# Int16 weight transposes moved from TensorE to a DMA queue in a pre-norm decoder layer

## The reference, cut to what matters

```python
x = x + attn(layernorm(x))                    # 16 query heads, 4 key/value heads, head size 16, rope, causal
x = x + cross(layernorm(x), ctx, mask)        # softmax(x ctx^T / 16, masked) @ ctx
xq  = quant_dequant(layernorm(x))             # per row: round(v / s) * s, s = max|v| / 127
gu  = xq @ quant_dequant(w_gate_up).T         # w_gate_up 1408 x 256, scale per output row
h   = silu(gu[..., :704]) * gu[..., 704:]
out = x + quant_dequant(h) @ quant_dequant(w_down).T    # w_down 256 x 704, scale per output row
```

## Time and profile before

| | us |
|---|---|
| median of three runs | 101.81 |
| lowest and highest of them | 101.38, 102.7 |
| the profiled execution | 102.22 |
| its span, first to last instruction | 100.4 |
| mean granted TensorE clock | 0.988 |

### The profile page before, as it was taken

The page is one execution under the profiler, slowest core; times in us unless marked ns, Lnnn a source line. Parts: engine busy times, 40 slices in busy tenths (PEclk is TensorE's granted clock), DMA queues, the critical chain, the costliest instruction groups (busy, mean ns, idle before and its releaser), DMA issues.

```text
span 100.4 us, 2487 instructions
## 1 busy us (share of the span) xinstructions
PE 92.1 (92%) x834; PEld 71.3 (71%) x834; DVE 75.4 (75%) x217; ACT 65.1 (65%) x175; POOL 61.5 (61%) x130
## 2 busy tenths in 40 slices
PE   5999699989999999999999999998999999999560
PEld 4788479766867787867877797776887977775220
DVE  5135979828999998697696669797878696998731
ACT  1403210489978677777787879689777897988420
POOL 5476666179922755976188674882489992872220
PEclk9999999999999999999999999999999999999995
DMA  2999999930000000000000000000000010021121
GB/s 35 368 342 421 416 407 415 351 98 3 0 7 3 0 3 0 7 0 0 7 0 0 0 0 7 3 0 0 0 0 0 7 52 3 0 104 52 52 104 52
DMA packets 4521, 8.34 MB, mean 83 GB/s; under 512 B 349, under 2 KB 3358, under 8 KB 4382
## 3 DMA queue, kind: packets, MB, share of 16 engines
q1 hardware_dynamic: 4272, 7.96, 21.6%
q10 hardware_dynamic: 238, 0.23, 0.7%
HBM read 7.15 MB, written 1.05 MB: 82 GB/s over the span
## 4 chain that ended last, share of the span: by engine, by line
PE 72%; DVE 13%; POOL 6%; issue 3%; ACT 3%; DVEq 0%; ACTq 0%; POOLq 0%
PE ps_s L456 11%; PE ps_r L263 8%; PE ps_q L304 6%; PE ps_y L538 4%; PE ps_r L290 4%; PE ps_y L372 3%; POOL gate_up L1169 3%; PE ps_r L399 3%; PE ps_s L352 3%; PE ps_s L328 3%; PE ps_x L388 2%; PE ps_q L312 2%; PE ps_y L364 2%; PE ps_s L339 2%; PE ps_s L482 2%
## 5 line engine op out<-in xcount | busy, mean ns | idle before, releaser
L1169 POOL TENSOR_TENSOR gate_up<-gate,up_row 128x704 f32<-128x704 f32 x7 | 11.9, 1699 | 6.6 <-ACT gate L738 5.0
L263 PE MATMUL ps_r<-warm 128*128 128x256 bf16 x58 | 9.5, 330 | 1.0 <-DVE warm L786 1.0
L1144 POOL TENSOR_TENSOR rot_c<-rot,b_rope 128x128 f32<-128x128 f32 x8 | 3.6, 456 | 9.1 <-DVE rot L861 9.1
L263 PEld LDWEIGHTS ps_r<-warm 128*128 128x128 bf16 x58 | 6.7, 120 | 3.1 <-DVE warm L786 1.0
L456 PE MATMUL ps_s<-gate_hi,x_int_T 128*128 128x352 f32 x28 | 7.7, 355 | 0.0
L884 DVE RECIPROCAL y_rsum<-ps_y 128x128 f32<-128x128 f32 x8 | 7.6, 950 | 0.1
L1200 POOL TENSOR_TENSOR y_out<-ffn,x_aug 128x256 f32<-128x256 f32 x7 | 4.8, 690 | 4.4 <-DVE ffn L1040 4.4
L538 PE MATMUL ps_y<-w_T,h_T 128*128 128x256 bf16 (+1 forms) x42 | 6.5, 275 | 0.9 <-DVE ffn L1040 0.8
L456 PE MATMUL ps_s<-up_int,x_int_T 128*128 128x352 f32 x32 | 6.8, 335 | 0.1
L456 PE MATMUL ps_s<-gate_lo,x_int_T 128*128 128x352 f32 x28 | 6.8, 323 | 0.0
L749 ACT ACTIVATE h_int<-hid,h_inv 128x704 int16<-128x704 f32 x7 | 6.1, 877 | 0.3 <-DVE h_inv L1035 0.3
(11 more groups left out here) (197 smaller groups left out, 290.6 us busy)
## 6 DMA issues: line engine op xcount, KB each, us to landing
ctxT<-in_ctxT SPq DMA_DIRECT2D x1, 1024.0 KB, 8.7
w_raw<-in_w SPq DMA_DIRECT2D x2, 512.0 KB, 11.2
ctx_aug<-in_ctx SPq DMA_DIRECT2D x1, 1024.0 KB, 17.1
out_x<-y_out SPq DMA_DIRECT2D x8, 128.0 KB, 1.7
x_aug<-in_x SPq DMA_DIRECT2D x1, 768.0 KB, 7.0
xT<-in_xT SPq DMA_DIRECT2D x1, 768.0 KB, 9.9
w_raw<-in_w SPq DMA_DIRECT2D x1, 704.0 KB, 14.8
x_first<-in_x_first SPq DMA_DIRECT2D x1, 416.0 KB, 4.5
```

The source lines that it names most:

```text
L263: nc.tensor.matmul(ps_r[:, 0:2 * T], warm[:, 0:P], warm[:, :], start=True, stop=True)
L1169: nc.gpsimd.tensor_tensor(gate_up[j % 2][:, :, :], gate[j % 2][:, :, :], up_row[:, :].rearrange("p (i f) -> p i f", i=2), ALU.mult).then_i ...
```

## The change

- SP's DMA queue transposes W1 and W2 with `dma_start_transpose`, block by block, as int16 (w1_int) and as bf16 (w2_bf). `transpose_gate`, `transpose_up`, `transpose_w2` and the spreads leave TensorE.
- The scales of W1 and W2 are stored as a row in DRAM and loaded back to all partitions by a broadcasting load.
- The gate half: GpSimd's new `scale_gate` widens the transposed integers and multiplies them with the row; `upper_gate` and `lower_gate` then work on SBUF, in two halves. gate_T and the row lie in the memory of w1_raw, so the last `quantise_w1` must be over before they are written.
- GpSimd's new `widen_w2` turns w2_int into bf16, after one memset of w2_bf.
- The context means use 8 columns in place of 60 and come in two halves of four sequences. One `keep_warm(7)` goes, another uses the bank ps_x.
- All five lists have a new order.

```diff
-    GT = -(-FF // P)
-    CM = 61
+    GT = FF // P
+    CM = 9
...
             sp.dma_start(ctx_aug[:, :, 0:D], ctx_in).then_inc(s["ctx_loaded"], 16)
+            done(sp, "w1_scale_done", len(W1_PARTS) - 1)
+            sp.dma_start(w1_row_dram.rearrange("(o p) -> p o", p=P), w1_scale[:, :], allow_slow_non_contiguous=True).then_inc(s["w1_row_stored"], 16)
+            done(sp, "w1_int_ready", 2)
+            sp.dma_start_transpose(w1_T[:, 0:GT + 1, :, :].rearrange("p o c t -> p (o c) t"),
+                                   w1_int[:, 0:GT + 1, :].rearrange("p o d -> p (o d)")).then_inc(s["gate_T_loaded"], 16)
+            done(sp, "w1_int_ready", 4)
+            sp.dma_start_transpose(w1_T[:, GT + 1:WT, :, :].rearrange("p o c t -> p (o c) t"),
+                                   w1_int[:, GT + 1:WT, :].rearrange("p o d -> p (o d)")).then_inc(s["up_T_loaded"], 16)
+            sp.wait_ge(s["w1_row_stored"], 16)
+            sp.dma_start(w1_row[:, :], w1_row_dram.unsqueeze(0).to_broadcast([P, 2 * FF])).then_inc(s["w1_row_loaded"], 16)
+            done(sp, "w2_scale_done", 0)
+            sp.dma_start(w2_row_dram.rearrange("(c p) -> p c", p=P), w2_scale[:, :], allow_slow_non_contiguous=True).then_inc(s["w2_row_stored"], 16)
+            sp.wait_ge(s["w2_row_stored"], 16)
+            sp.dma_start(w2_row[:, :], w2_row_dram.unsqueeze(0).to_broadcast([P, D])).then_inc(s["w2_row_loaded"], 16)
+            for c in range(DC):
+                done(sp, "w2_bf_ready", c)
+                sp.dma_start_transpose(w2_T[:, :, c * P:(c + 1) * P], w2_bf[:, c, :]).then_inc(s[f"w2_T_{c}_loaded"], 16)
             for j in range(B):
...
+            def upper_gate(c):
+                done(act, "gate_T_ready", c)
+                nc.scalar.copy(gate_hi[:, c, :], gate_T[:, c, :]).then_inc(s["gate_hi_ready"], 1)
+            def evacuate_up(c):
+                act.wait_ge(s["gate_T_loaded"], 16)
+                act.wait_ge(s["up_T_loaded"], 16)
+                nc.scalar.copy(up_int[:, c, 0:FL], w1_T[:, GT, c, FL:P])
+                nc.scalar.copy(up_int[:, c, FL:FF].rearrange("p (o t) -> p o t", t=P), w1_T[:, GT + 1:WT, c, :]).then_inc(s["up_int_ready"], 1)
...
+            def lower_gate(c):
+                done(dve, "gate_T_ready", c)
+                done(dve, "gate_hi_ready", c)
+                nc.vector.tensor_tensor(gate_lo[:, c, :], gate_T[:, c, :], gate_hi[:, c, :].bitcast(F32), ALU.subtract).then_inc(s["gate_lo_ready"], 1)
...
+            def scale_gate(c):
+                done(pool, "w1_int_ready", 4)
+                pool.wait_ge(s["gate_T_loaded"], 16)
+                pool.wait_ge(s["w1_row_loaded"], 16)
+                nc.gpsimd.tensor_copy(gate_T[:, c, 0:GT * P].rearrange("p (o t) -> p o t", t=P), w1_T[:, 0:GT, c, :])
+                nc.gpsimd.tensor_copy(gate_T[:, c, GT * P:FF], w1_T[:, GT, c, 0:FL]).then_inc(s["gate_T_widened"], 1)
+                done(pool, "gate_T_widened", c)
+                nc.gpsimd.tensor_tensor(gate_T[:, c, :], gate_T[:, c, :], w1_row[:, 0:FF], ALU.mult).then_inc(s["gate_T_ready"], 1)
+            def widen_w2(c):
+                done(pool, "w2_int_ready", c)
...
+                nc.gpsimd.tensor_copy(w2_bf[:, c, 0:FF], w2_int[:, c, :]).then_inc(s["w2_bf_ready"], 1)
```

More of the change, by code:

```diff
@@ L287, in mean_ctx, with mean_ctx_half @@
                 pe.wait_ge(s["ctxT_loaded"], 16)
-                for j in range(B):
+                mean_ctx_half(0)
+            def mean_ctx_half(half):
+                means = ps_r[:, 0:B * CM].rearrange("p (b n) -> p b n", n=CM)
+                for j in range(half * B // 2, (half + 1) * B // 2):
                     for c in range(DC):
@@ L532, in down @@
                     done(pe, "x1_ready", B - 1)
-                    done(pe, "w2_ready", DC - 1)
+                    for c in range(DC):
+                        pe.wait_ge(s[f"w2_T_{c}_loaded"], 16)
                 bank_free(pe, "ffn_ready", j)
@@ L559, in _ @@
             pe.wait_ge(s["warm_ready"], 1)
[L560 to L563, removed]
-            transpose_gate(1, "gate_lo_ready", 0); transpose_q_max(1); mask_other_keys(1); transpose_qk(2)
@@ new lines, in _ @@
+            rotate_sum(4); residual_2(0); max_scores(3); amax_x(0); invert_sums(2); max_cross(1)
+            step_x(0); invert_x(0); normalise_y(2); bias_cross(1); rotate(5); residual_1(2); invert_cross_sum(1)
+            rotate_sum(5); max_scores(4); invert_sums(3); lower_gate(0); residual_2(1); normalise_y(3)
+            amax_x(1); max_cross(2); bias_cross(2); rotate(6); step_x(1); invert_x(1); residual_1(3)
+            invert_cross_sum(2); rotate_sum(6); max_scores(5); invert_sums(4); lower_gate(1); normalise_y(4)
@@ new lines, in _ @@
+            residual_2(2); max_cross(3); bias_cross(3); amax_x(2); step_x(2); invert_x(2); residual_1(4)
+            rotate(7); max_scores(6); invert_cross_sum(3); rotate_sum(7); invert_sums(5); residual_2(3)
+            normalise_y(5); max_cross(4); bias_cross(4); residual_1(5); max_scores(7); invert_cross_sum(4)
+            amax_x(3); invert_sums(6); normalise_y(6); step_x(3); invert_x(3); max_cross(5); bias_cross(5)
+            residual_1(6); residual_2(4); invert_cross_sum(5); amax_x(4); step_x(4); invert_x(4); invert_sums(7)
@@ new lines, in _ @@
+            finish_gate(0); residual_2(5); max_cross(6); bias_cross(6); normalise_y(7); amax_x(5)
+            invert_cross_sum(6); step_x(5); invert_x(5); residual_1(7); finish_gate(1); residual_2(6)
+            max_cross(7); bias_cross(7); hidden(0); amax_h(0); amax_x(6); scale_h(0); invert_h(0); hidden(1)
+            step_x(6); invert_x(6); amax_h(1); invert_cross_sum(7); scale_h(1); invert_h(1); hidden(2)
+            residual_2(7); amax_h(2); amax_x(7); scale_h(2); invert_h(2); step_x(7); invert_x(7); hidden(3)
@@ L1081, in _ @@
+            add_residual(7)
         @block.gpsimd
@@ L1097, in _ @@
             pool.wait_ge(s["v_zero"], 1)
+            nc.gpsimd.memset(w2_bf[:, :, :], 0.0).then_inc(s["w2_bf_zero"], 1)
             nc.gpsimd.memset(v_pad[:, :, :, DH:DH + 1], 1.0).then_inc(s["ones_ready"], 1)
@@ new lines, in _ @@
+            scale_rope(3); centre_x(3); centre_x(4); centre_x(5); scale_rope(4); scale_rope(5); centre_ctx(0)
+            centre_x(6); rstd_2(0); centre_ctx(1); rotate_c(3); scale_rope(6); centre_x(7); centre_ctx(2)
+            centre_ctx(3); rotate_c(4); scale_gate(0); rstd_2(1); centre_ctx(4); scale_rope(7); rotate_c(5)
+            scale_gate(1); rstd_2(2); rotate_c(6); whole_x2(0); centre_ctx(5); widen_w2(0); rstd_2(3)
+            centre_ctx(6); widen_w2(1); rotate_c(7); rstd_2(4); scale_x(0); whole_x2(1); scale_x(1); whole_x2(2)
```

258 lines of the change are left out of this document (82 added, 176 removed).

## The result

| us | before | after |
|---|---|---|
| median of four runs each, same chip | 102.25 | 108.09 |
| lowest and highest | 101.38, 103.34 | 107.79, 110.67 |
| ratio of the times, 95% interval | | 1.060 [1.050, 1.070] |

The change makes the kernel 6% slower. The forecast was 98.2 with a range of 94.8 to 105.5: wrong in sign and outside the range. The profile of after is of its longest run, 110.67, with a mean granted clock of 0.883; the others (spans 106.0 to 106.6) have 0.896 to 0.923, so its rows carry 2 to 3 us more than the median.

A forecast was written before the change was run, and what follows sets the result against it. TensorE, busy 92% of the span, was taken as the bound between 30 and 90 us. Profiled 102.2 - 0.3 (lead at rotate(5)) - 4.0 (TensorE) + 0.5 (GpSimd) = 98.4, adjusted to the runs' median 98.2; range 94.8 to 105.5.

The forecast's parts named there:

- Part 1: Start, until rotate(3): less TensorE work puts rotate(2) near 18.8; lead of 3.0 us at rotate(3) and rotate(4).
- so 0.3 us: In the start: context-mean products of 8 columns in place of 60, bounded between nothing and 1.6 us, taken to save 0.3.
- Part 2: GpSimd in the middle: 5.9 us more work, not the bound by its sum; by its order rotate(5) starts near S + 4.2.
- S: Start of scale_gate(0) on GpSimd: forecast 33.5, break-even 33.8, every microsecond above that lost one for one.
- Part 3: When S is, by scale store, transposes and row load in SP's queue: low end 31, high end 39.7, taken as 33.5.
- rival B: Transposes or 4-byte store late, S near 39.7, rotate(5) 5.9 us late: 104.6 us, deciding from S = 39.3; chance 0.25.
- rival A: Everything on time: S = 31, rotate(5) at 35.2, lead 2.8 us, time 95.9 us; chance 0.16.
- Part 4: From rotate(5) to the end: TensorE loses 4.0 us of pieces, 0.5 us given back for GpSimd's added blocks.
- All of them pieces of the chain: After rotate(5): TensorE's removed spreads, up transposes and w2 transposes lie on the chain, counted as 4.0 us gained.
- most of it fits: GpSimd after rotate(5): scale_gate(1) and widen_w2, 5.7 us, mostly fit beside its other work; 0.5 us given back.
- rival C: GpSimd's order sets the middle's pace; TensorE's 2.24 us there become waits, only w2's 1.78 gained: 100.1 us; chance 0.19.

The follow-up runs named there:

- e1: The changed kernel with the context means back at the old width (CM = 61 in place of 9): 105.19 us, ratio 1.034 to the kernel before.
- e6: e5 with rstd_2(1) moved ahead of scale_gate(0) on GpSimd and evacuate_up(0) behind evacuate_qk(4) on ScalarE: 97.81 us, ratio 0.958.
- e4: The changed kernel with CM = 61 and no scale stores, rows loaded from W1's input instead: 99.36 us, ratio 0.974.
- e5: The changed kernel with CM = 61, scales transposed on TensorE and stored as 512-byte rows, W1's store behind the first transpose in SP's queue: 99.94 us, ratio 0.977.
- e8: The changed kernel with CM = 61 and W1's scales stored as 128 runs of 44 bytes, not 1408 elements of 4: 99.61 us, one run.
- e9: e6 without the products and most copies of scale_gate(1) and without most of W2's widening on GpSimd: 97.61 us, ratio 0.956.
- e10: The kernel before with TensorE's up and W2 pieces after rotate(5) mostly cut and nothing put on another engine: 102.19 us, ratio 0.990.

## Why the prediction was wrong, step by step

- **Part 1, the start.** The removed pieces did what was said: with the clock whole, rotate(2) comes at 18.21 (e1) and 18.48 (e6) for the 18.8 forecast, rotate(4) at 29.13 (e6) for 30. The step that failed is "so 0.3 us" for the 8-column products. They saved nothing (117 and 118 ns each), and they brought the clock down to 0.50: a loss of about 2.7 us in after, 1.6 in before. The row behind the 0.3 was misread, too: the four products at 7.29 have 64 columns in the trace, not 32, so it said nothing of narrower ones. The prediction looked for a lower clock only where TensorE is idle, as the earlier trace rows show it at the end.
- **Part 2, GpSimd.** Right, with the blocks a little dear: scale_gate 2.65 us for 3.05 (42.61 to 45.26), widen_w2 0.77 for 1.3, rotate(5) at S + 3.7 for S + 4.2. The S + 3.7 holds in after, e1, e4, e5 and e8, where scale_gate(0) waits for its row, with S from 31.6 to 42.6; moving rstd_2(1) forward, and evacuate_up(0) with it, was worth 1.2 us at rotate(5) (e6).
- **Part 3, S.** The step that failed is the 4-byte store. It was bounded by the packets of ScalarE's queue, 4.1 us and 1.7 to landing; it took 11.4. A row of 1 KB packets says nothing on a store of 4-byte elements, and the bound should have been called open at the top; rival B did so, but for the transposes' pieces and not for the store. With the store mended everything else was at the low end: S 31.6 (e8), 32.0 (e5, e6), where rival A had 31 and the forecast 33.5. The int16 transposes cost 1.3 to 1.6 us of SP's time to issue (up to 2.5 when the first is issued early, as in e5 and e9) and, where no 4-byte store stands in front, 4.0 to 4.7 us to land; the bf16 ones 2.7 to 2.8, against 1.7 for an out_x of 128 KB. The page Advanced Engine Details and Errata of the Trainium skill (X-Bar Transpose (TRN2)) has them as fast as regular DMAs. By the forecast's byte rate a plain transfer of 328 or 393 KB would land in 2.5 to 2.7 us, so they were slower than that; no run has a plain transfer of that size to set beside them. The S = 31 that goes with the page was still nearer than 33.5.
- **Part 4, the sum after rotate(5).** Both terms failed. "All of them pieces of the chain" was taken as if a piece of the chain were worth its length: 4.0 us were counted and 2.2 came, in after as in e6. One of the two up transposes, at 59.89, is not in the chain of before at all. In before itself, cutting 2.6 us gives 0.8 by the last gate and between nothing and 1 us in the time (e10). And "most of it fits", 0.5 us, was 1.3 in e6 and 2.3 in after. In e6 most of it comes not by the blocks named there, scale_gate(1) and widen_w2 (e9), but by scale_gate(0) in front of rotate_c(5). That is rival C's mechanism at a smaller size: the net was 0.85 in e6 and -0.2 in after, for 3.5.
- **Rival B** named the place and the direction: its point of decision, S = 39.3, was passed. Its 104.6 was short because S was 42.6 and not 39.7, because the clock loss of Part 1 came on top, and because it still took 3.5 us back after rotate(5). In e1, without the clock's fall in the start, rotate(5) is 3.6 late; B's sum gives 102.2 + 3.6 - 3.5 = 102.3, and the profiled execution took 104.5. It also expected that TensorE would run dry and its clock fall: it did (40 to 45 us above, 3.30 of 5 busy at 0.75).
- **The number 98.2** is near e6's 97.81 only by errors that cancel: S 1.5 us earlier and two lists reordered, which puts rotate(5) at 34.5 and not 37.7, against 2.7 us that Part 4 had too much.

## What to carry to other kernels

A store whose pieces are single elements is to be priced as unknown and large, whatever its bytes; transpose such a column on TensorE first and store rows. Here 8 columns per product in place of 60 saved no time and cost the clock of the microseconds behind them: where products are narrowed, look at the granted clock after, even if TensorE stays busy. And that pieces lie on the chain says where time passes, not what their removal gives: look beside each for the engine that would have held the next step anyway. A block of some microseconds on an engine with room by its sum still costs what it puts in front of a token's small steps: here the order of two lists alone was worth 2 us (e5 to e6).

## What the runs showed of the hardware that was not expected

- A DRAM store of 1408 4-byte elements lands after 10.8 to 11.4 us, one of 256 elements after 8.5 to 9.5, with the DMA share at 0.00 for two microseconds of it; 5.5 KB in 44-byte pieces after 1.4.
- An f32 product of 128x128 weights takes 118 ns with 60 columns and 117 with 8, and 16 to 32 of the narrow ones in a row bring the granted clock from 1.00 to 0.50 although TensorE is busy (without a gap in after).
- An int16 copy of 640 elements by GpSimd takes 0.72 us, 1.1 ns an element, where the product w_q of before took 1.89.
